# Two parts of a value projection moved from behind the attention's first scores to ahead of them

## What is computed

```
q = ((seq2 + b_self) @ Wq + bq)                # 16 heads of 32
k = (concat(seq1 + b_prev, seq2 + b_self) @ Wk + bk)
v = (concat(seq1, seq2) @ Wv + bv)
score_prev = einsum('bhqd,bhkd->bhqk', q, k[:, :, :l1]) * SCALE      # masked by length
score_self = (q * k[:, :, l1:]).sum(-1, keepdims=True) * SCALE
weights = softmax(concat(score_prev, score_self), -1)
attn = weights[..., :-1] @ v[:, :, :l1] + weights[..., -1:] * v[:, :, l1:]
x = x + attn @ Wo + bo
```

## Time and profile before

| | us |
|---|---|
| median of 3 runs (1278.84 to 1279.36) | 1279.25 |
| the profiled execution, its own time | 1278.37 |
| the profiled execution, span | 1276.6 |
| TensorE busy in it | 1208.0 |
| VectorE busy | 903.3 |
| ScalarE busy | 839.2 |
| GpSimd busy | 511.7 |

### The profile page before, as it was taken

How to read it: one execution, slowest core, us unless ns; L and a number is a source line. 1 busy time by engine, 2 the same in 40 slices (tenths; PEclk the granted TensorE clock), 3 DMA queues, 4 the chain that set the end, 5 groups by cost and what they waited for, 6 DMA issues and landing times.

```text
span 1276.6 us, 18385 instructions
## 1 busy us (share of the span) xinstructions
PE 1208.0 (95%) x6289; PEld 479.2 (38%) x6289; DVE 903.3 (71%) x1500; ACT 839.2 (66%) x1763; POOL 511.7 (40%) x445
## 2 busy tenths in 40 slices
PE   7999999999999999999989999999999999999995
PEld 4332443324442343323433244332443324433253
DVE  7876578766786658865598656986569855787556
ACT  5898348864588635985369853798438883388732
POOL 6505364044632366132751417605175053650212
PEclk9999999999999999999999999999999999999996
DMA  6304445136343273432633435424354154451110
GB/s 218 83 8 143 91 90 110 62 90 123 69 108 82 63 133 67 99 111 50 117 81 86 124 58 108 87 67 143 51 108 107 34 143 82 93 104 58 40 34 33
DMA packets 215322, 113.47 MB, mean 89 GB/s; under 512 B 166498, under 2 KB 189374, under 8 KB 215230
## 3 DMA queue, kind: packets, MB, share of 16 engines
q1 hardware_dynamic: 215168, 112.30, 39.0%
q10 hardware_dynamic: 62, 0.01, 0.0%
HBM read 40.81 MB, written 8.40 MB: 39 GB/s over the span
## 4 chain that ended last, share of the span: by engine, by line
PE 48%; ACT 23%; DVE 20%; issue 4%; DMA 1%; POOL 1%; SPq 1%; POOLq 0%; ACTq 0%; DVEq 0%
ACT banks L865 15%; PE bank L505 13%; PE banks L505 11%; PE banks L1539 9%; PE bank L1555 8%; DVE nmx L1147 7%; ACT big L921 3%; PE bank L1504 2%; DVE x L1105 2%; DVE prod L1136 2%; ACT bank L948 1%; PE banks L1467 1%; PE bank L1565 1%; SPq L684 1%; DVE tiles_in L1098 1%
## 5 line engine op out<-in xcount | busy, mean ns | idle before, releaser
L865 ACT ACTIVATE banks<-banks,nmx 128x512 f32<-128x512 f32 x512 | 342.6, 695 | 69.9 <-DVE nmx L1147 69.7
L1147 DVE TENSOR_REDUCE nmx<-banks 128x1 f32<-128x512 f32 x512 | 324.5, 682 | 22.3 <-PE banks L1467 21.8
L921 ACT ACTIVATE big<-banks 128x1024 f32<-128x1024 f32 x256 | 248.1, 1021 | 50.6 <-PE banks L1539 50.0
L505 PE MATMUL bank<-fT,w_hi 128*128 128x512 f16 x768 | 255.8, 379 | 0.6 <-DVE fT L1063 0.6
L1467 PE MATMUL banks<-KQ 97*128 97x512 f16 x512 | 196.6, 384 | 33.5 <-ACT banks L865 28.0
L625 POOL TENSOR_TENSOR x<-x,bo_rows 128x512 f32<-128x512 f32 x32 | 40.4, 1294 | 322.8 <-DMA x<-in_x_dram 322.8
L505 PE MATMUL bank<-fT,w_lo 128*128 128x512 f16 x384 | 145.4, 379 | 0.0
L1539 PE MATMUL banks<-KQ 98*128 98x512 f16 x512 | 142.0, 382 | 2.5 <-DVE q L1168 0.2
L542 POOL TENSOR_TENSOR split<-tiles_in,ones 128x512 f16<-128x512 f32 x56 | 61.5, 1098 | 200.8 <-DMA xT<-split 197.8
L1555 PE MATMUL bank<-big,V 128*32 128x512 f32 x1024 | 136.4, 605 | 0.0
L865 ACT ACTIVATION_READ_ACCUMULATOR banks<-banks,nmx 128x1 f32 x512 | 123.4, 241 | 0.0
(11 more groups left out here) (168 smaller groups left out, 1773.1 us busy)
## 6 DMA issues: line engine op xcount, KB each, us to landing
KQ<-half SPq DMA_DIRECT2D x384, 64.0 KB, 2.0
tiles_in<-in_x_dram SPq DMA_DIRECT2D x32, 256.0 KB, 8.0
x<-in_x_dram SPq DMA_DIRECT2D x8, 1024.0 KB, 5.4
out_dram<-x SPq DMA_DIRECT2D x32, 256.0 KB, 2.3
tiles_in<-in_fside_BxSxS_dram SPq DMA_DIRECT2D x28, 256.0 KB, 2.7
hT<-in_L_cond_W_dram SPq DMA_DIRECT2D x8, 256.0 KB, 3.9
w<-in_L_cond_W_dram SPq DMA_DIRECT2D x8, 256.0 KB, 4.0
b2r<-in_L_cond_b_dram SPq DMA_DIRECT2D x8, 256.0 KB, 4.4
```

The lines of the kernel that those rows point to most:

```text
L505: mm = eng.matmul(out_ap, pairs[n][0], pairs[n][1], start=(first and n == 0), stop=(last and n == len(pairs) - 1))
L865: eng.activation(bank(step, i)[:, v, :], bank(step, i)[:, v, :], ACT.Exp, bias=nmx[:, t, h:h + 1], accum_out=esum[:, t, h:h + 1]).then_inc ...
L921: eng.activation(big[:, n % 2, 2 * u:2 * u + 2, :], bank(step)[:, :, :], ACT.Exp).then_inc(read(step), 1)
L1147: eng.tensor_reduce(nmx[:, t, h:h + 1], bank(step, i)[:, v, :], AX_X, ALU.max, negate=True).then_inc(max_done, 1)
```

## The change

One constant is another: of the six parts of ("V", 3) only one is now issued between the scores of block 0 and block 1, where there were three. The other two parts take slots at the end of `order_mid`.

```
-LATE_PARTS = 3
+LATE_PARTS = 1
```

## The result

The changed kernel takes 1284.36 us in the median of 6 runs (1283.93 to 1285.42), the kernel before 1279.23 in 6 runs of the same kind. The ratio is 1.0042, with a 95% interval from 1.0031 to 1.0054: slower by 5.1 us, where 5.3 were forecast. The profiled execution took 1283.93, its span is 1281.8 against 1276.6, so 5.2 more.

What follows compares the result with a forecast made beforehand. The prediction took TensorE's and ScalarE's waits for each other in the attention as the bound; 6 x 0.72 + 0.70 + 0.30 = 5.32 us, taken as 5.3, brought the 1279.25 median to 1284.6, range 1281.7 to 1286.2.

Steps and rivals of the forecast that it cites:

- What bounds: In the attention, TensorE's and ScalarE's waits for each other at the edited place count, not TensorE's 95% busy time.
- A slot of 0.217, four are 0.87: Ahead of block 0's scores: each moved matmul takes 0.217 us, so four delay the first exponential by 0.87.
- ScalarE sets the second pair: At block 1: ScalarE, free at 247.96, starts the second two exponentials there instead of at 247.24, 0.72 us late.
- Two chains, and the even one dies at block 7: Within an attention: even blocks late by 0.87, odd by 0.72; the extra 0.15 ends at block 7, 0.72 goes on.
- The sum: Over eight boundaries: six at 0.72 (4.32), the third 0.70, the first 0.30, together 5.32 us.
- The new wait of 0.68: On TensorE ahead of block 1's scores, from 246.40 to 247.08: 0.68 us, with the clock priced at nothing.
- Absorption (1): Behind the attention, work not tied to its end absorbs the delay at half the boundaries: 1281.9 us, chance 0.13.
- The free order (2): TensorE is the bound and its order is free, since it does the same work: 1279.25 us, chance 0.09.
- The DMA as releaser (3): The shift row's DMA releases block 0's scores, so the four fill a wait: gain 1.6, 1277.6 us, chance 0.05.
- The even chain's 0.86 (4): The even blocks' delay, forecast as 0.87, survives the attention: at most 6.7 us, so 1286.0, chance 0.05.
- The sign of a longer period: Expected in the profile if right: each period longer by 0.7 us; a period of unchanged length would show it wrong.
- The rule on PSUM banks: Skill rule that independent matmul groups use different banks; taken literally it prices the four at 0.87, 6.9 us in all.

Runs made afterwards that it cites:

- two ahead: Kernel before with two of the six late matmuls put ahead of block 0's scores, four left behind them: ratio 1.0016, 2.0 us slower.
- the four left out: Kernel before without four of the six late matmuls of the last value projection (parts 3 and 4): ratio 0.9988, 1.5 us less.
- the pair of kernels with GpSimd's wait: Kernel before and changed kernel, each with GpSimd's next-x splits waiting for VectorE's first head group: ratios to the kernel before 0.9980 and 1.0032.
- eight or ten late matmuls: Kernel before with late matmuls, from the second sequence on, six and two (ratio 0.9988) or six, two and two (0.9992), the twos between score halves.
- twelve: Kernel before with all twelve matmuls of the last value step behind block 0's scores: ratio 1.0031, 4.0 us slower.
- eight late matmuls in one place: Kernel before with eight instead of six late matmuls between the scores of block 0 and block 1: ratio 1.0008.

## Why the prediction was right

Its steps, one by one:

- **What bounds.** Right: the same work of TensorE cost 1.5 in one place and 6.6 in the other.
- **A slot of 0.217, four are 0.87.** Right: block 0 is later by 0.86, and by 0.84 in the third attention, whose wait for the DMA is gone.
- **ScalarE sets the second pair.** Right in kind: the four exponentials follow each other without a gap. Mis-sized: I took 1.95 from the chain for two exponentials. That is from the first start to the second end; the next one starts before that end. Four in a row take 3.77, and blocks 0 and 1 are 1.83 apart. Block 1 is later by 0.59, not 0.72.
- **Two chains, and the even one dies at block 7.** Right for the even one: blocks 2, 4 and 6 are 0.86 late, block 7 and all behind it 0.73. Wrong for the odd one, which I let run by itself: from block 1's second half TensorE goes on to block 3's scores with hardly a pause, so block 3 follows block 2 by 1.96 and is 0.73 late, where block 1 was 0.59. Its 0.73 is the even chain's 0.86 less a pause of 0.13 on TensorE between the halves of block 2's scores. The wait there was 0.46 in the kernel before and is 0.18 in the changed one, and the step between the halves' first matmuls fell from 0.57 to 0.44 (first row the kernel before, second the changed one):

```profile
249.23 0.11 PEld L1539 LDWEIGHTS banks<-KQ 98*128 98x128 f16 x2 [0.46 <-ACT big L921]
...
249.97 0.25 PEld L1539 LDWEIGHTS banks<-KQ 98*128 98x128 f16 x2 [0.18 <-ACT big L921]
```

The other runs have the same difference: with two ahead block 0 is 0.43 late and block 3 0.30, with the four left out 0.00 and -0.14. The prediction gave back 0.15, ScalarE's gap ahead of block 1; what is given back is this pause of 0.13. That the two sizes are so close is luck, so the 0.72 is right as a number and only in part as a path.
- **The sum.** 0.73 where 0.72 stood, 0.71 at the third attention where 0.70, 0.31 at the first where 0.30; at block 9 5.37 where 5.32. The measured 5.1 is as near as that only because the movements behind block 9, which the sum hasn't, cancel to 0.2. (The upper end adds 0.62 where its own numbers give 0.63; the 6.7 stays.)
- **The new wait of 0.68.** From 246.33 + 0.22 to 247.23 it is 0.68. The granted clock is 1.00 at all eight boundaries of the changed kernel (at the second from 244 to 250), so the clock cost nothing there, as said.
- **Rivals.** Absorption (1) is seen inside an attention once, in the sixth, where 0.52 of the 0.72 is gone at block 10, because the kernel before has its stretched distance of 3.02 there; in the pair of kernels with GpSimd's wait the whole 5.38 reaches the ends of the attentions. The free order (2) fell with the four left out. The DMA as releaser (3): in the changed kernel no load of block 0's scores waits for it; with eight or ten late matmuls, where TensorE gets there earlier, the row is waited for twice in eight, and with twelve each time. The even chain's 0.86 (4) ends at block 7.
- **The sign of a longer period.** "Each period longer by 0.7" did not come out one by one: from maxima to maxima the seven periods are longer by 0.26 to 1.41, since the stretches between the attentions move too. The attentions themselves show it.
- **The rule on PSUM banks.** The Trainium skill, Perfetto Trace Analysis, Optimizing Tensor Performance, says that the evacuation of one group should overlap the next group's matmuls. The prediction's estimate for the four, with the rule taken literally, was 6.9; the run with the four left out makes it 6.6 ahead of the scores, but 1.5 under cover too, so 5.1 between the two places.

What I had not in view is the phase of VectorE against GpSimd behind block 9. It moved single attentions by -0.53 to +0.22 between the two profiles, and happened to give back 0.41 in sum.

## What to carry to other kernels

Work that an in-order engine issues right behind the first piece of a pipeline is nearly free as long as the consumer of that piece is busy (here 1.5 of 6.9); the same work ahead of the piece costs nearly its whole time (6.6), since the consumer starts later by it. So start the consumer first, fill the time until its first buffer comes free, and spread the filling over all the waits and not only the first. More filling than the waits hold only moves the wait to the consumer: eight late matmuls in one place gave nothing. And a pair's time in a chain is not the step between pairs: take it from rows with several instructions in a run.

## What the runs showed of the hardware

Exponentials of 128 x 1024 are 1.02 us long but follow each other every 0.92: the next one begins ahead of the end of the one before (3.77 for four).

VectorE's steps on SBUF operands grow beside GpSimd's splits: L1238 from 0.69 to 1.66, L1240 from 0.49 to 1.15, L1242 from 0.75 to 1.52, while L1234, which reads one input from PSUM, stays at 0.68. GpSimd's split grows with them, from 1.04 to 1.49. Not every overlap lengthens VectorE's step: in the changed kernel's row above L1238 stayed at 0.69, and the split beside it took 1.56. The Trainium skill, GPSIMD Engine Reference, Specifications, says that the two engines share SBUF interfaces and that VectorE's instructions with two SBUF inputs or in a two-port mode contend. The trace agrees for L1238 and L1242, which have two SBUF inputs; which mode L1240 runs in isn't shown here. The one wait that keeps the splits of the next x off the first group's steps went with 2.6 us by the ratio, of which the traces show 0.63 behind block 9.
